# A recommendation tower on one Trainium2 core: two sets of row and vector buffers, tiles written out, the pairs of three slots by a product

## What is computed

```python
e = jnp.stack([tbl_0[ids[:, 0]], ..., tbl_25[ids[:, 25]]], axis=1)
sd = jnp.einsum('bfd,bd->bf', sparse_values, dense_features)
ss = jnp.einsum('bfd,bgd->bfg', sparse_values, sparse_values)
pairs = ss[:, iu, ju]
z = jnp.concatenate([dense_features, sd, pairs], axis=1)
h = jnp.concatenate([z, r_dense_features], axis=1)
h = jnp.maximum(h @ W_top1 + b_top1, 0.0)
h = jnp.maximum(h @ W_top2 + b_top2, 0.0)
y = h @ W_top3
```

## Time and profile before

| | us |
|---|---|
| median of three runs | 134.19 |
| the three runs | 133.56, 134.19, 215.45 |
| span of the profiled execution (the page gives no other time of it) | 178.9 |
| TensorE busy | 127.8 |
| VectorE busy | 79.5 |
| ScalarE busy | 86.8 |
| GpSimd busy | 78.4 |

### The profile page before, as it was taken

How to read it: one execution, slowest core, us unless ns; L and a number is a source line. 1 busy time by engine, 2 the same in 40 slices (tenths; PEclk the granted TensorE clock), 3 DMA queues, 4 the chain that set the end, 5 groups by cost and what they waited for, 6 DMA issues and landing times.

```text
span 178.9 us, 2260 instructions
## 1 busy us (share of the span) xinstructions
PE 127.8 (71%) x752; PEld 112.7 (63%) x752; DVE 79.5 (44%) x217; ACT 86.8 (49%) x240; POOL 78.4 (44%) x87
## 2 busy tenths in 40 slices
PE   2499996236994986968450799685343999887794
PEld 1357764113883985967450799675333999877793
DVE  3799850008960498042402770050408623389201
ACT  4679916007971499530502766030508672289210
POOL 4777777735777005757771027477740000000000
PEclk9999999755799699999876558999555569999699
DMA  4985543980212001111211002111210000000000
GB/s 132 243 189 165 150 130 67 375 295 16 60 46 59 16 0 29 48 38 50 59 44 29 4 0 59 44 44 44 59 44 0 0 0 0 5 0 0 0 4 0
DMA packets 4801, 11.39 MB, mean 64 GB/s; under 512 B 2244, under 2 KB 2244, under 8 KB 4664
## 3 DMA queue, kind: packets, MB, share of 16 engines
q1 hardware_dynamic: 2232, 6.03, 11.3%
q0 software_dynamic: 2560, 5.25, 11.1%
HBM read 11.27 MB, written 0.00 MB: 63 GB/s over the span
## 4 chain that ended last, share of the span: by engine, by line
PE 35%; another core or an unknown queue 32%; DVE 17%; issue 5%; ACT 5%; DMA 3%; SPq 1%; ACTq 0%; DVEq 0%
PE ps_gram L291 11%; PE ps_h_bank L378 8%; DVE dots L501 7%; PE ps_gram L360 7%; DMA dense<-in_r_dense_features 3%; ACT dots L613 3%; DVE vecs L474 3%; PE ps_dve L322 2%; DVE dots L505 2%; PE ps_act L322 2%; PE ps_gram L390 2%; DVE dots L498 2%; PE ps_h_bank L331 1%; DVE one_hot L455 1%
## 5 line engine op out<-in xcount | busy, mean ns | idle before, releaser
L265 POOL DMA_INDIRECT rows<-in_tbl,ids_sb x80 | 77.6, 970 | 53.1 <-issue 22.6
L360 PE MATMUL ps_gram<-vecs 128*128 128x104 f32 x256 | 39.6, 323 | 27.2 <-ACT dots L617 17.9
L360 PEld LDWEIGHTS ps_gram<-vecs 128*128 128x128 f32 x256 | 37.6, 235 | 29.3 <-DVE dots L505 19.0
L378 PE MATMUL ps_h_bank<-dots,w_dots 128*128 128x128 f32 x192 | 26.2, 305 | 3.4 <-DVE dots L505 1.8
L378 PEld LDWEIGHTS ps_h_bank<-dots,w_dots 128*128 128x128 f32 x192 | 26.0, 222 | 3.7 <-DVE dots L505 3.7
L455 DVE TENSOR_TENSOR one_hot<-ps_gram,row_id 125x1024 fp32r<-125x1024 f32 (+1 forms) x18 | 19.0, 1098 | 17.2 <-remote 15.1
L291 PE MATMUL ps_gram<-one_hot,table_hi 125*128 125x512 f32 x48 | 22.0, 480 | 2.5 <-issue 2.3
L613 ACT COPY dots<-ps_gram 32x48 f32<-32x48 f32 x96 | 22.9, 239 | 1.3
L501 DVE COPY dots<-ps_gram 32x48 f32<-32x48 f32 x96 | 22.8, 238 | 1.6
L498 DVE COPY dots<-ps_gram 32x16 f32<-32x16 f32 x32 | 5.7, 177 | 39.9 <-remote 26.0
L610 ACT COPY dots<-ps_gram 32x16 f32<-32x16 f32 x32 | 5.8, 182 | 34.5 <-remote 26.0
(11 more groups left out here) (41 smaller groups left out, 101.0 us busy)
## 6 DMA issues: line engine op xcount, KB each, us to landing
table<-in_tbl SPq DMA_DIRECT2D x6, 448.0 KB
w_dots<-in_w_dots SPq DMA_DIRECT2D x1, 1536.0 KB
rows<-in_tbl,ids_sb POOLq DMA_INDIRECT x80
w_dense<-in_w_dense SPq DMA_DIRECT2D x1, 512.0 KB
w<-in_W_top SPq DMA_DIRECT2D x1, 512.0 KB
table<-in_tbl SPq DMA_DIRECT2D x6, 52.0 KB
dense<-in_r_dense_features SPq DMA_DIRECT2D x1, 256.0 KB, 5.3
ids_sb<-in_ids SPq DMA_DIRECT2D x1, 52.0 KB, 1.9
```

Source lines behind the costliest of these rows:

```text
L265: pool.indirect_dma_start(out=rows[:, slot - EARLY, :], out_offset=None, in_=ins[f"tbl_{f}"], in_offset=bass.IndirectOffsetOnAxis(ap=ids[: ...
L360: last = pe.matmul(ps_gram[:, part % 2 * BANKS + g // PER_BANK, c0:c0 + COLS], vecs[:, p0:p0 + QUADS, :], vecs[:, p0:p0 + QUADS, 1:SLOTS], ...
L378: last = pe.matmul(bank[:, o, :], w1_dots[:, j, (o0 + o) * P:(o0 + o + 1) * P], dots[:, j, :], start=False, stop=(j == STEPS - 1), skip_gr ...
```

## The change

The changed kernel

- has two sets of `rows` and of `vecs`, so that tile t + 1 is gathered and transposed while tile t is in its Gram stage; a gather waits for transposes of two tiles earlier. The cold slots are five batches of four, which alternate between the two PSUM banks over all tiles. `dots` has its own part for each tile;
- writes the four tiles out, without a loop, with layers 1 to 3 of tile 0 between the Gram parts of tile 1; layer 3 of each tile now stands with its layers 1 and 2; these write PSUM banks of their own, not the Gram's;
- makes the pairs of slots 0 to 2 by three elementwise products over all samples on VectorE in the prelude, summed over partitions by TensorE (`triangle`) and copied into `dots`. The spare copies go, and a Gram product has 96 columns instead of 104;
- places a sample's column in `vecs` in another order, so that a fold copy writes runs of eight neighbouring samples;
- has rings of three for `table`, `table_hi` and `table_lo` (before four, six and six), and sends the weights in ten pieces, each after the one before has landed, between the tables.

```diff
-        rows = sb("rows", [P, len(COLD), D])
+        rows = sb("rows", [P, ROW_SETS, len(COLD), D])
-        vecs = sb("vecs", [P, P, PITCH])
-        dots = sb("dots", [P, STEPS, P])
+        vecs = sb("vecs", [P, 2, P, PITCH])
+        dots = sb("dots", [P, TILES, STEPS, P])
...
+        def places(t, s0, s1):
+            return vecs[:, t % 2, :, s0:s1].rearrange("d (g s) f -> d f s g", s=QUADS)
+        def quarters(x):
+            return x.rearrange("d f (s g) -> d f s g", s=QUADS)
...
             src = ps_gram[:, part % 2 * BANKS:(part % 2 + 1) * BANKS, 0:PER_BANK * COLS].rearrange(
-                "a k (g s c) -> a k g s c", g=PER_BANK, s=QUADS)
-            dst = dots[:, :, :].rearrange("a j (h k g s) -> a h s k g j", h=PARTS, k=BANKS, g=PER_BANK)
+                "a k (g s c) -> a s c k g", g=PER_BANK, s=QUADS)
             for s in samples:
-                if spare:
-                    yield (dst[0:PITCH, part, s, :, :, 0:COPIES],
-                           src[PITCH * s:PITCH * (s + 1), :, :, s, 0:COPIES])
...
+                p0 = PITCH * s + PER_PART * part
+                dst = dots[:, t, :, p0:p0 + PER_PART].rearrange("a j (k g) -> a j k g", k=BANKS)
+                for q in (1, 2, 3, 0):
+                    n = PITCH if q > 0 else SLOTS
+                    yield (dst[PITCH * q:PITCH * q + n],
+                           src[PITCH * s:PITCH * s + n, s, STEPS * q:STEPS * (q + 1)])
...
+            def weight_piece(n, dst, src):
+                if n >= 1:
+                    sp.wait_ge(s_w, 16 * n)
+                sp.dma_start(dst, src).then_inc(s_w, 16)
...
-                    if t >= 1:
-                        pool.wait_ge(s_tp, (t - 1) * NB + g + 1)
+                    if t >= ROW_SETS:
+                        pool.wait_ge(s_tp, (t - ROW_SETS) * NB + g + 1)
...
+            def triangle():
+                pe.wait_ge(s_sel, 1)
+                pe.wait_ge(s_prod, 2)
+                pe.wait_ge(s_dve_read, DVE_USES.index("tri"))
+                for i in range(len(TRI)):
+                    last = pe.matmul(ps_dve[0:PITCH, :, :].rearrange("a t p -> a (t p)"),
+                                     sel[:, i * PITCH:(i + 1) * PITCH], prod[:, i, :],
+                                     start=(i == 0), stop=(i == len(TRI) - 1))
+                last.then_inc(s_tri, 1)
...
+            def layer_1(t, bank, o0, s_done):
                 for o in range(OC1 // 2):
+                    chunk = slice((o0 + o) * P, (o0 + o + 1) * P)
+                    pe.matmul(bank[:, o, :], w1_fold[:, chunk], early[:, 0, t * P:(t + 1) * P],
+                              start=(o == 0), stop=False, skip_group_check=True)
+                    if o == 0:
+                        pe.wait_ge(s_fold_dve, t * PARTS + PARTS)
+                        pe.wait_ge(s_fold_act, t * PARTS + PARTS)
+                    for j in range(STEPS):
+                        last = pe.matmul(bank[:, o, :], w1_dots[:, j, chunk], dots[:, t, j, :],
...
+            gram(1, 0)
+            layer_1_act(0)
+            gram(1, 1)
...
+            def products():
+                dve.wait_ge(s_dve_read, 1)
+                dve.wait_ge(s_pick_read, 2)
+                nc.vector.tensor_mul(prod[:, 0:2, :], early[:, 1:3, :],
+                                     early[:, 0:1, :].to_broadcast([P, 2, BATCH])).then_inc(s_prod, 1)
+                nc.vector.tensor_mul(prod[:, 2, :], early[:, 1, :], early[:, 2, :]).then_inc(s_prod, 1)
```

More of the change, by code:

```diff
@@ L62 @@
 RING = 3
-TABLE_RING = 4
 EARLY = 1 + NHOT
@@ L179, in build, with on_dve, dve_uses_to @@
         s_out = sem("s_out")
[L181 to L186, removed]
+        DVE_USES = ["dense", (0, 0), "tri"] + [(n // NB, n % NB) for n in range(2, TILES * NB, 2)]
+        ACT_USES = [(n // NB, n % NB) for n in range(1, TILES * NB, 2)]
+        def on_dve(t, g):
+            return (t * NB + g) % 2 == 0
+        def dve_uses_to(t):
+            return max(n for n, u in enumerate(DVE_USES) if not isinstance(u, str) and u[0] <= t) + 1
@@ new lines, in gram @@
+            def gram(t, part):
+                if part == 0:
+                    pe.wait_ge(s_early, t + 1)
+                    pe.wait_ge(s_dve_read, dve_uses_to(t))
+                    pe.wait_ge(s_act_read, act_uses_to(t))
+                if t == 0 and part == 1:
+                    pe.wait_ge(s_pick_read, NHOT)
+                if t * PARTS + part >= 2:
+                    pe.wait_ge(s_fold_dve, t * PARTS + part - 1)
+                    pe.wait_ge(s_fold_act, t * PARTS + part - 1)
+                for g in range(PER_PART):
+                    p0 = QUADS * (part * PER_PART + g)
+                    c0 = g % PER_BANK * COLS
+                    last = pe.matmul(ps_gram[:, part % 2 * BANKS + g // PER_BANK, c0:c0 + COLS],
+                                     vecs[:, t % 2, p0:p0 + QUADS, :], vecs[:, t % 2, p0:p0 + QUADS, FIRST_B:SLOTS],
+                                     start=True, stop=True)
+                last.then_inc(s_gram, 1)
@@ new lines, in _, with fold @@
+            dve.wait_ge(s_tri, 1)
+            nc.vector.tensor_copy(dots[0:PITCH, :, 0, :], ps_dve[0:PITCH, :, :]).then_inc(s_dve_read, 1)
+            nc.vector.memset(vecs[:, 1, :, SLOTS:PITCH], 0.0).then_inc(s_pad, 1)
+            read_transposed(0, 2)
+            read_transposed(0, 4)
+            def fold(t, part):
+                dve.wait_ge(s_gram, t * PARTS + part + 1)
+                for dst, src in fold_blocks(t, part, FOLD_DVE):
+                    last = nc.vector.tensor_copy(dst, src)
+                last.then_inc(s_fold_dve, 1)
@@ L595, in _ @@
             read_picked(NHOT - 1)
+            read_transposed(0, 3)
             act.wait_ge(s_pick_read, NHOT)
[L598 to L621 removed]
@@ L622, in act_tile, with fold, relu_1 @@
+            def fold(t, part):
+                act.wait_ge(s_gram, t * PARTS + part + 1)
+                for dst, src in fold_blocks(t, part, FOLD_ACT):
+                    last = nc.scalar.copy(dst, src)
+                last.then_inc(s_fold_act, 1)
+            def relu_1(t):
+                if t == 0:
+                    act.wait_ge(s_small, 48)
                 act.wait_ge(s_h1_act, t + 1)
```

565 lines of the change are left out of this document (319 added, 246 removed).

## The result

The changed kernel takes 144.07 us (median of four runs, 143.19 to 145.27) against 135.66 for the kernel before, timed beside it: a ratio of 1.073 [1.064, 1.081]. The forecast was 136.3 with a range to 141.5.

A forecast was written before the change was run, and what follows sets the result against it. It took stages without overlap, TensorE and the folds' engines waiting for each other, as the bound. First Gram at 45.3, later tiles' at 59.0, 89.9 and 114.9, plus 21.7 gave 136.6, less 0.3: 136.3 us, range 130.5 to 141.5.

The forecast's parts named there:

- TensorE at full speed in the Gram products: Gram products of every tile: each of a tile's four parts takes 1.9 us on TensorE, 7.6 us in all.
- the stage of tile 1: Gram of tile 1 with layers 1 to 3 of tiles 0 and 1: TensorE bounds it, 30.9 us against 22.9 before.
- the last tile: From tile 3's first Gram product to the end: 8.9, 12.06 and 0.7 us, so 21.7 instead of 23.9.
- My third rival: TensorE at its lower clock in layer 1 of tiles 2 and 3: two such layers at 9 us give 140; chance 0.13.
- the prelude: Work before the first Gram product: 3.45 us longer than 41.9, so that product starts at 45.3 us.
- the stage of tile 0: First Gram of tile 0 to that of tile 1: ScalarE is the longest, 1.9 + 11.8 us after 45.3.
- the scale: Whole kernel: the typical run is the profiled execution without its late signals, 134.5 against 134.19 us, 0.3 off.
- Fold copies: Copies in each tile's folds: 0.21 us each, eight a part and engine instead of ten, so 1.7 us a part instead of 2.4.
- Tile 1's start: First Gram product of tile 1: starts at 59.0 us, set by ScalarE; the gathers would allow 56.9.
- The stage of tile 2: Tile 2's Gram, folds and layers, serial as before: 25.0 us, so tile 3's Gram starts at 114.9.
- The gathers: Faster rival: with two row sets GpSimd runs through its 80 gathers and sets the end, 127 us; chance 0.19 of below 131.5.
- Folds at 238 ns: Slower rival, in every stage: scattered reads keep a fold copy at 238 ns and the end comes at 139 us; chance 0.25.

## Why the prediction was wrong

**The step that failed: TensorE at full speed in the Gram products.** "Gram 4 x 1.9 = 7.6" in the stage of tile 1 and the 1.9 in "1.9 + 6.8 + 0.2 = 8.9" of the last tile are full-speed figures. Behind the waits of 4.27 and 1.26 us ahead of tile 1, and behind those of 1.15 and 1.33 ahead of tiles 2 and 3, part of the products ran at 1.2 GHz: 1.7, 1.6 and 3.2 us more on the Gram alone, and 1.3 on the products that follow in tile 1. Filling the waits gave 5.2 us back, with some clock lost at layer 1 of tile 2 in its place. My third rival had the mechanism but put it at layer 1, with a chance of 0.13 and a price of 3 to 4 us; layer 1 of tile 2 ran at full speed, and the Gram products paid. With the waits filled the span is 136.4; the sum said 136.6. That it comes so near is partly luck: the prelude (44.4 against 45.3) and the stage of tile 1 (29.4 against 30.9) were shorter than in the sum, the stage of tile 0 (15.3 against 13.7) was longer.

**The second step: the scale.** "The typical run is this execution without its late signals, 0.3 us off" took a span for a time; 1.9 us lie outside. 136.6 + 1.9 is 138.5, the filled run 138.9.

**The terms.** The prelude was wrong twice, to 45.3 instead of 44.12: it began 1.5 us too early, and the change added 0.8, not 3.45. VectorE's loop gained far more than the 0.2 I counted. In the kernel before, without late signals, and then in the changed one:

```profile
30.84 1.22 DVE L455 TENSOR_TENSOR one_hot<-ps_gram,row_id 125x1024 fp32r<-125x1024 f32 x1 [2.12 <-PE ps_h_bank L279]
...
35.35 1.12 DVE L474 COPY vecs<-ps_dve 128x512 f32<-128x512 f32 x1 [2.16 <-PE ps_dve L322]
36.31 2.34 DVE L455 TENSOR_TENSOR one_hot<-ps_gram,row_id 125x1024 fp32r<-125x1024 f32 x2
```

```profile
24.21 1.08 DVE L491 COPY vecs<-ps_dve 128x512 f32<-128x512 f32 x1 [1.93 <-PE ps_dve L326]
...
33.73 2.35 DVE L500 TENSOR_TENSOR one_hot<-ps_gram,row_id 125x1024 fp32r<-125x1024 f32 x2
```

The last one-hot ended at 38.65 before and at 36.08 after: two long waits for TensorE became one. Fold copies (0.21 against 0.200 and 0.191) and reads (1.06 against 1.05 and 1.065) were right. By the rule on SBUF lines of the Trainium skill ("Advanced Engine Details and Errata", section "Memory Cachelines"), the estimate, worked out from the rows, was 0.197, and the trace agrees (0.200 and 0.191). The PSUM half, which the section states for matmuls, would have left the copy at 0.238; that did not show here, although the reading side is scattered. Tile 1's start was right to 0.8 us by luck: rows came at 57.42, not 55.2, and TensorE waited for them, not for ScalarE. The stage of tile 2 is 25.2 in the changed kernel, against 25.0, and that too is partly luck: the two copies on ScalarE are worth 2.0 rather than 2.8, and half-speed Gram products made up for a layer 1 that I took too long (6.1 us, where I had 6.7 and 0.7). The last tile has 0.8 us of output transfer that I did not have (2.2 us against 1.4).

**The rivals.** The gathers were a rival on the fast side for a wrong reason: 21.7 us of GpSimd's waits came with the late signals. In the undisturbed profiles GpSimd runs through, so a second set of rows had nothing to free; its last gather starts at 104 to 106 us in every order that was profiled with all 80 gathers, its rows arrive some 2.2 us later, and the kernel before already started its last Gram at 109. What an overlap could win was the tail behind that, and the changed kernel paid for it with waits. Folds at 238 ns fell with the first group row.

**What the loss is.** By ratios: 1.073, with the waits filled 1.034, and with the two ScalarE copies behind the folds 1.001. The two bring it back to the kernel before. The third figure comes from another chip than the second. The filled run with one set of rows, timed on that chip, had 1.016, so the copies' share may be anything from 1.5 to 3.3%; the profiles give 3.7 us for it (spans of 136.4 and 132.7). What the folds gain, 1.9% by themselves, does not show in the changed kernel on top; how its prelude, output transfer and longer chain of layers share that was not measured apart. By the ratios no version of the changed kernel beat the kernel before; the new order of columns alone did, by 1.9%.

## What to carry to other kernels

Before an overlap is built, look in an undisturbed profile at when the slowest serial supply (here one gather each 1.25 us) delivers its last piece, and compare it with the start of the work that needs it; if both coincide, only a shorter supply or less work behind that point helps. A profile with late signals whose sender the trace does not know is not a measure of waits, and its stages can add up to the right time by accident. On TensorE, price every new wait twice: by its length, and by products behind it that may run at half clock; filling it with idle products is a quick test of which it was.

## What was not expected of the hardware

TensorE's clock stayed at 0.50 well after work had resumed: in the changed kernel through 117.30 to 123.00, although it was busy from 117.39 on. The wait's length alone does not tell: the Gram products of tiles 2 and 3 lost the clock behind waits of 1.15 and 1.33 us, while layer 1 ran at 1.00 behind 3.18 us in the changed kernel and started at half speed behind 3.15 in the filled one. The Trainium skill, "TensorE: Matmul & The Clock Gate", section "HAM oscillation — how this bites in real kernels", describes long waits for a transfer between groups of products, each of which makes the next group start at half clock. The trace agrees for the rows of tile 1 (4.27 us, then 0.50). In the filled run a wait of 3.15 us for a copy out of PSUM had the products behind it slow as well, and in the two runs of the new column order the Gram products behind a wait for rows were slow once (5.42, behind 2.52 us) and once not (3.79, behind 1.49 us).

The output's transfer of 2 KB, with its time to landing as the last figure, in the kernel before and in the changed one:

```profile
out_y<-y SPq DMA_DIRECT2D x1, 2.0 KB, 1.4
```

```profile
out_y<-y SPq DMA_DIRECT2D x1, 2.0 KB, 2.2
```

It took 2.2 to 2.5 us in every version of the changed kernel and 1.4 in every version of the old one. The weight pieces are not the cause (2.4 without them); the cause stays open.
